# Equal destinations by ±1 products on TensorE and ScalarE, and extra bf16 matmuls into an unread PSUM bank, in a two-stage graph network

## The reference

```
h = relu(layernorm(x))                       # stage one
gate = silu(edge_attr @ W1.T + b1) @ W2.T + b2 + adapt(type[src], type[dst])
msg  = gate * h[dst] * (cutoff(edge_weight) * node_vec[dst])
agg  = segment_sum(msg, src) / clip(segment_sum(node_vec[dst], src), 1e-8)
x    = x + layernorm(h + agg) * gamma + beta
h = relu(layernorm(x))                       # stage two
h1 = relu(h @ weight1[r] + bias1);  h2 = h1 @ weight2[r]     # r: type of the edge
agg = segment_sum(h2[src, r] * norm, dst)
x   = x + relu(agg + bias2)
```

## Time and profile before

| | |
|---|---|
| median of 3 runs | 1531.99 us (1529.84 to 1539.69) |
| span of the profiled execution | 1526.4 us (the profile gives no time of its own for that launch beyond the span) |
| DVE / PE / POOL / ACT busy | 1319.3 / 1130.4 / 1026.1 / 668.1 us |
| stage one, its last adds, stage two, last pass | 0 to 689, to 743, to 1417, to 1526 us of the span |
| granted TensorE clock | two levels, 1.0 (2.4 GHz) and 0.5 (1.2 GHz), mixed in every stage |

### The profile page before, as it was taken

The page is one execution under the profiler, slowest core; times in us unless marked ns, Lnnn a source line. Parts: engine busy times, 40 slices in busy tenths (PEclk is TensorE's granted clock), DMA queues, the critical chain, the costliest instruction groups (busy, mean ns, idle before and its releaser), DMA issues.

```text
span 1526.4 us, 20418 instructions
## 1 busy us (share of the span) xinstructions
PE 1130.4 (74%) x5198; PEld 831.4 (54%) x5198; DVE 1319.3 (86%) x3932; ACT 668.1 (44%) x1627; POOL 1026.1 (67%) x809
## 2 busy tenths in 40 slices
PE   5889899989999899881068888887878887775000
PEld 2767677777777777771035555555555555554000
DVE  6999999999989998980289999998989899888599
ACT  2444444544445444540155555555555555554000
POOL 7655667777877787566667787877777777766000
PEclk9666655655556655655575656655565556666555
DMA  7999986666666656642445666555555555554899
GB/s 225 307 324 327 328 236 157 153 146 143 142 166 149 149 139 143 155 101 11 100 120 143 166 167 156 140 138 137 136 139 127 132 131 138 138 127 81 328 400 398
DMA packets 154391, 268.73 MB, mean 176 GB/s; under 512 B 73818, under 2 KB 90411, under 8 KB 153380
## 3 DMA queue, kind: packets, MB, share of 16 engines
q1 hardware_dynamic: 78228, 223.53, 43.8%
q0 software_dynamic: 68992, 24.64, 18.5%
q10 hardware_dynamic: 7056, 19.27, 3.1%
HBM read 194.33 MB, written 112.55 MB: 201 GB/s over the span
## 4 chain that ended last, share of the span: by engine, by line
PE 34%; DVE 20%; DMA 19%; POOL 12%; issue 10%; ACT 3%; SPq 1%; POOLq 0%; DVEq 0%; ACTq 0%
PE ps_m L572 10%; POOL agg L485 8%; DMA t<-agg,src_all 6%; PE ps_m L661 6%; PE ps_qs L572 6%; DMA lows<-low 4%; PE ps_k L647 3%; DVE same L858 2%; DMA agg<-y,once 2%; DMA agg<-ysq,once 2%; DVE t L1074 2%; DVE x L1070 2%; PE ps_k L559 2%; PE ps_k L560 2%; PE ps_qs L610 1%
## 5 line engine op out<-in xcount | busy, mean ns | idle before, releaser
L521 POOL DMA_INDIRECT agg<-sums,once x196 | 312.7, 1595 | 103.5 <-issue 79.8
L443 POOL DMA_INDIRECT nodes<-in_table,dst_all x196 | 194.9, 995 | 102.2 <-issue 51.7
L512 POOL DMA_INDIRECT t<-agg,src_all x196 | 191.5, 977 | 66.1 <-issue 53.9
L572 PEld LDWEIGHTS ps_m<-msg,same 128*128 128x128 f32 x980 | 200.8, 314 | 29.0 <-issue 29.0
L572 PE MATMUL ps_m<-msg,same 128*128 128x48 f32 x980 | 208.5, 398 | 1.0 <-issue 1.0
L647 PE MATMUL ps_k<-h_t,rw_sb 56*128 56x256 f32 x588 | 122.7, 536 | 114.0 <-ACT hid L742 91.3
L572 PEld LDWEIGHTS ps_qs<-msg,same 128*128 128x128 f32 x980 | 183.6, 289 | 2.1 <-DVE msg L950 2.1
L572 PE MATMUL ps_qs<-msg,same 128*128 128x49 f32 x980 | 180.7, 363 | 2.0 <-DVE msg L950 2.0
L485 POOL DMA_INDIRECT agg<-x,once x84 | 137.4, 1635 | 43.9 <-issue 21.7
L647 PEld LDWEIGHTS ps_k<-h_t,rw_sb 56*128 56x128 f32 x588 | 62.9, 242 | 157.1 <-ACT hid L742 115.2
L559 PE MATMUL ps_k<-types_lo,low_hot 128*128 128x392 bf16 x196 | 95.7, 488 | 52.7 <-DVE low_hot L833 51.0
(11 more groups left out here) (149 smaller groups left out, 2620.2 us busy)
## 6 DMA issues: line engine op xcount, KB each, us to landing
agg<-in_both SPq DMA_DIRECT2D x14, 2758.0 KB, 15.3
t<-agg SPq DMA_DIRECT2D x49, 784.0 KB, 5.3
kept<-kept_out SPq DMA_DIRECT2D x49, 404.0 KB
kept_in<-kept SPq DMA_DIRECT2D x49, 404.0 KB, 3.5
agg<-bias_rows SPq DMA_DIRECT2D x49, 384.0 KB
out<-t ACTq DMA_DIRECT2D x49, 384.0 KB, 5.8
rows<-in_src_rows SPq DMA_DIRECT2D x49, 256.0 KB, 4.2
rows<-in_dst_rows SPq DMA_DIRECT2D x49, 256.0 KB, 3.2
```

The lines of the kernel that those rows point to most:

```text
L443: pool.indirect_dma_start(nodes[s][:, t, :], None, table, bass.IndirectOffsetOnAxis(ap=dst_all[:, c:c + 1], axis=0)).then_inc(nodes_in[b % ...
L512: pool.indirect_dma_start(t2[b % T2S][:, t, :], None, wide, bass.IndirectOffsetOnAxis(ap=src_all[:, c:c + 1], axis=0)).then_inc(ends_in[b ...
L521: pool.indirect_dma_start(agg1, bass.IndirectOffsetOnAxis(ap=once1[b % LAG1][:, t:t + 1], axis=0), sums1[b % LAG1][:, t, :], None, compute ...
L572: last = mm(ps[:, t * width:(t + 1) * width], kept_same[:, at:at + P], m[:, v, :], start=(v == t), stop=(v == TILES - 1))
```

## The change

1. `keep_clock(ps, n)`: n matmuls of the bf16 identity with itself repeated, 128x512, into a PSUM bank that nobody reads (`ps_idle`, `ps_idle1`, `ps_spare`). Stage one gets ten per round, stage two six.
2. In stage two DVE no longer builds `same`. SP loads the keys of four blocks at once, each broadcast to 32 partitions; DVE shifts and masks so that partition p holds bit p mod 32 (`bits_done`), and makes it +1 or -1 in bf16 (`signs`), once in four rounds each. PE multiplies those signs (`key_dots`, contraction over 32 partitions), so that equal keys give 32; a second product adds -64 where the row's edge is later. ACT evicts with `relu(x - 31)` into `same` and sums the rows into `ahead1` (`same1_copy`).
3. Once `same` comes from ACT, `turned1` and `once1` of a block are computed one DVE round later (`d = b - 3`).

```diff
-POOL_SET = 15
+POOL_SET = 16
+GROUP = 4
+NBITS = 32
+APART = -2.0 * NBITS
...
+        signs = [upto[:, :].bitcast(BF16)[:, k * BE:(k + 1) * BE] for k in range(2)]
...
+        ps_idle = ps_k[0][:, 1, :]
+        ps_idle1 = ps_k[1][:, 1, :]
+        ps_spare = ps_k[1][:, 0, :]
+        ps_dots = [ps_k[1][:, 0, 0:P], ps_k[1][:, 0, P:3 * P], ps_k[1][:, 1, 0:3 * P], ps_k[1][:, 0, 0:BE]]
...
-            def load_rows1(b):
-                need(sp, S["same1_done"], b - 1)
-                sp.dma_start(rows[b % 2][:, :], dst_rows[b:b + 1, :].to_broadcast([P, BE])).then_inc(rows_in[b % 2], 16)
...
+            def load_keys(k):
+                need(sp, S["signs_done"], k - 1)
+                for q in range(GROUP):
+                    b = min(k * GROUP + q, NBLOCK - 1)
+                    sp.dma_start(rows[k % 2][q * NBITS:(q + 1) * NBITS, :],
+                                 dst_rows[b:b + 1, :].to_broadcast([NBITS, BE])).then_inc(keys_in[k % 2], 16)
...
+            spin = ident_bf[:, :].unsqueeze(1).to_broadcast([P, TILES, P])
+
+            def keep_clock(ps, n):
+                for _ in range(n):
+                    mm(ps, ident_bf[:, :], spin, start=True, stop=True)
...
-            def sums_within(ps, width, kept_same, m):
+            def sums_within(ps, width, kept_same, m, ps_spin):
                 for t in range(TILES):
                     for v in range(t, TILES):
+                        if v == t and t > 0:
+                            keep_clock(ps_spin, 1)
...
             for b in range(NBLOCK):
+                keep_clock(ps_idle, 3)
                 if b + 1 < NBLOCK:
                     lookup(b + 1, 0)
                     lookup(b + 1, 1)
+                keep_clock(ps_idle, 1)
...
                 last.then_inc(S["gate_done"], 1)
+                keep_clock(ps_idle, 1)
                 if b + 1 < NBLOCK:
                     h1(b + 1)
+                    keep_clock(ps_idle, 1)
                     centred(b + 1)
+                    keep_clock(ps_idle, 1)
...
+            def key_dots(b, t):
+                at = slice(b % GROUP * NBITS, (b % GROUP + 1) * NBITS)
+                bits = signs[b // GROUP % 2]
+                mm(ps_dots[t], bits[at, t * P:(t + 1) * P], bits[at, 0:(t + 1) * P], start=True, stop=False)
+                mm(ps_dots[t][:, t * P:(t + 1) * P], ident_bf[:, :], later[:, :], start=False, stop=True).then_inc(S["dots_done"], 1)
...
                         if k == 1:
-                            need(pe, S["relu1_done"], e)
+                            need(pe, S["same1_done"], TILES * e)
...
+                    need(pe, S["relu1_done"], min(e + 1, NBLOCK))
+                    sums_within(ps_sums1, H, same[f % 2], msg1, ps_idle1).then_inc(S["sums1_done"], 1)
                 if e < NBLOCK:
+                    pe.wait_ge(S["signs_done"], e // GROUP + 1)
+                    pe.wait_ge(S["relu1_done"], e + 1)
+                    for t in range(TILES - 1):
+                        key_dots(e, t)
                     need(pe, S["m1_copied"], e)
...
                     last.then_inc(S["m1_done"], 1)
+                    pe.wait_ge(S["same1_done"], TILES * e + 2)
+                    keep_clock(ps_spare, 3)
+                    key_dots(e, TILES - 1)
...
+            def same1_copy(b, t):
+                act.wait_ge(S["dots_done"], b * TILES + max(t + 1, 2))
+                if t == 0:
+                    need(act, S["sums1_done"], b - 1)
+                    need(act, S["turned1_done"], b)
+                n = P * (t + 1)
+                A(same[b % 2][:, place(t):place(t) + n], ps_dots[t], ACT.Relu, bias=1.0 - NBITS,
+                  accum_out=ahead1[:, t:t + 1]).then_inc(S["same1_done"], 1)
...
                 if 0 <= f < NBLOCK:
+                    same1_copy(f, 0)
+                    same1_copy(f, 1)
+                    same1_copy(f, 2)
                     act.wait_ge(S["m1_done"], f + 1)
...
                     nc.scalar.copy(msg1_t[:, :], ps_m[:, 0:BE // 2]).then_inc(S["m1_copied"], 1)
+                    same1_copy(f, 3)
...
-                if 0 <= d < NBLOCK:
-                    dve.wait_ge(rows_in[d % 2], 16 * (uses(NBLOCK - 1 - d % 2, 2) + uses(d, 2)))
-                    need(dve, S["sums1_done"], d - 1)
-                    same_up_to(d, dst_all, ahead1).then_inc(S["same1_done"], 1)
+                if 0 <= b < NBLOCK + GROUP - 1 and b % GROUP == 1:
+                    dve.wait_ge(S["bits_done"], b // GROUP + 1)
+                    V.tensor_scalar(signs[b // GROUP % 2], rows[b // GROUP % 2][:, :], 2.0, -1.0, ALU.mult,
+                                    ALU.add).then_inc(S["signs_done"], 1)
...
+                if 0 <= b < NBLOCK and b % GROUP == 0:
+                    k = b // GROUP
+                    dve.wait_ge(keys_in[k % 2], 16 * GROUP * uses(k, 2))
+                    need(dve, S["dots_done"], GROUP * TILES * (k - 1))
+                    V.tensor_scalar(rows[k % 2][:, :], rows[k % 2][:, :], bit_of[:, :], 1, ALU.logical_shift_right,
+                                    ALU.bitwise_and).then_inc(S["bits_done"], 1)
```

29 lines of the change are left out of this document (19 added, 10 removed).

## The result

The changed kernel takes **1625.72 us** (median of 4 runs, 1619.85 to 1631.19) against 1530.91 for the kernel before (4 runs, 1517.64 to 1539.69): ratio **1.062, 95% interval 1.056 to 1.069, slower**. Forecast were 1515 us and a range of 1484 to 1548. The profiled execution took 1630.99 us, its span is 1628.5 against 1526.4.

What follows compares the result with a forecast made beforehand. POOL's chain of adds was taken to bound stage one, a two-round loop over POOL, DVE and PE stage two. Terms -5 - 3 - 5 - 4 + 0.5 = -16.5 on 1526.4, plus 5.6, gave 1515 us, range 1484 to 1548.

Steps and rivals of the forecast that it cites:

- Item 3: Stage two's loop of two rounds: path averages 10.8 us, a round 13.2 us against 13.34, -5 us, bounds -20 and +54.
- the path of 11.07 us: Stage two, from DVE's L973 over the sums and L661 to the end of L781: 8.6 us at full clock, 13.7 at half.
- the 14.85 us to the landing: Stage two, from POOL's first add of a block over its gathers to the landing DVE awaits; kept at 14.85 us.
- Items 1 and 2: Stage one: first fourteen rounds shorten towards 12.65 us, -5 us; three more blocks of POOL's adds go at 9.46 us, -3 us.
- rival B: Nothing gained: transfers hold the first fourteen rounds, stage two's full rounds pay for the half ones; 1529 us, chance 0.19.
- Item 4: PE's own round in stage two: 10.7 us plus 4.1 at half clock, 14.8, more than the round; not added to the sum.
- Item 5: PE's waits in stage two: some 1.6 us between L661 and h2_t at full clock, hidden before the gather lands; nothing added.
- Item 6: Start and end of stage two, about two rounds where DVE's saved 1.97 us count: -4 us, bounds -6 and 0.
- C: Stage two slower: half-clock sums every round lengthen the path to 13.7 us, PE's own round to 14.8; 1574 us, chance 0.13.
- A: Clock holds in both stages, by the rule that bursts without long gaps keep full clock; -42, 1490 us, chance 0.25.
- D: Extra matmuls don't move the clock, PE bounds stage one, 4.3 us more a round; about 1780 us, chance 0.03.
- DVE's L973 no longer waits: Sign in stage two's profile for C: first adds over 13.9 us apart and no DVE wait for the gather's landing.

Runs made afterwards that it cites:

- late_all: Changed kernel with key products behind the h2 transposes, large loads held back to the next asum, and no extra matmuls; 1562.3 us, ratio 1.024.
- gap_late3: gap_late with three instead of six extra matmuls in PE's wait ahead of the last rw1 matmuls; 1639.0 us, ratio 1.073.
- loads_late: Changed kernel with loads of kept values and wide rows held back until the next round's asum has begun; 1572.4 us, ratio 1.029.
- dots_late: Changed kernel with three tiles' key products behind the h2 transposes, the last one and three extra matmuls behind the message transposes, evictions later; 1567.4 us, ratio 1.021.
- b_dots: Kernel before with the large loads held back and six bf16 key-product matmuls on constants, results unused, ahead of rw2 each round; 1563.2 us, ratio 1.029.
- s1_only: Kernel before with only stage one's ten extra bf16 matmuls a round, stage two unchanged; 1519.5 us, ratio 0.995.
- turn_first: loads_late with the h2 transposes ahead of the eviction wait, the three extra matmuls behind rw2 and the last key product; 1588.8 us, ratio 1.041.
- gap_moved: loads_late with stage two's extra matmuls replaced by six in PE's wait for relu0 ahead of the last rw1 matmuls; 1550.1 us, ratio 1.016.
- gap_late: gap_moved with the key products and evictions placed as in dots_late; 1519.6 us in one run, 1547.4 to 1560.0 in three others, no ratio given.
- split: Kernel before with stage two's sums in another PSUM bank, their copy no longer waiting for the rw2 matmuls; 1512.4 us, ratio 0.990.
- b_loads_late: Kernel before with the same held-back loads as loads_late; 1513.9 us, ratio 0.993.

## Why the prediction was wrong

- **Item 3, the path of 11.07 us, is the step that failed.** It had the ends about right, 8.6 us at full clock (9.23 in one waiting round that had it) and 13.7 at half (measured 13.56), and then took an average, 10.8. But the loop of two rounds goes through waiting rounds alone, and in these PE waits longest ahead of its sums: in all 20 rounds in which it waited 3.3 us or more ahead of L684, the sums were at half clock. The wait is not the only way to slow sums: late_all and gap_late3 have them in every round without it. The prediction even names that wait ("longer than that after which the clock was low") and still gives it half of the rounds. The rounds with fast sums have slack, and their gain went nowhere. `key_dots` was taken at 1.3 us at half clock and took 1.62, the three extra matmuls in the sums at 1.3 and took 0.87; that 13.56 is so close to 13.7 is in part these two misses against each other.
- **Also item 3: the 14.85 us to the landing were taken as fixed.** They became 14.5 to 18.7. The longer path moved the gathers against the end of `x2`, which starts 1.19 MB of loads; nothing in the sum had a row for that. loads_late prices it at 3.3 points. Taking the key products off the path was worth 4.1 (dots_late) and putting them on it cost the kernel before 3.6 (b_dots); the parts overlap and do not add up to the 6.2. Rows to ask it of were there: in the kernel before the landing already varied between 1.6 and 2.7 us by the same distance.
- **Items 1 and 2, -8 us, came to nothing.** The clock (0.89) and the rounds after the fourteenth (12.7) are as said, but the first add came at 211.47, not near 207, and the last block as before. The first fourteen rounds went only from 13.48 to 13.34 us with the DMA share at 0.96, rival B's reason (s1_only, with the same extra matmuls there, has 13.8). POOL's adds have their own pace.
- **Item 4**: PE's round is no bound; it idles 3.3 us and more ahead of L684 in most waiting rounds, 4.48 in the one shown. Only in gap_late3 did it become one.
- **Item 5, PE's queue behind L703, costed at nothing.** DVE's one-hot waits for L665 up to 2.4 us, in rounds without a landing to wait for. turn_first could not price it. ACT's row sums are an instruction of their own of 196 ns, four a round, not nothing; they run beside L703.
- **Item 6** can't be read apart.
- **The rivals.** C came true in its first mechanism, with 13.56 us for its 13.7, at a chance of 0.13. Its 1574 us lacked the landing; that loads_late, where this is gone, takes 1572 is luck, as C's loop has rounds of 14.7 us and loads_late 14.08. Its second mechanism, PE's own round as the bound, did not come. Its sign "DVE's L973 no longer waits" was wrong: DVE waited longer. A and B were out, D too. Of the rule that spoke for A: in gap_moved the clock is at half where a gap of 3.11 us is left, in gap_late, where none is, at full. In gap_late3 none is left either, and the clock is at half in all of stage two's sums, so the rule is not enough; what else decides stays open. What I failed to ask was which rounds have the gap.

## What to carry to other kernels

- If a loop's length is set by one kind of round, cost the change in that kind and not on average. Here PE's clock was at half in just the rounds in which PE had waited longest.
- When a path gets longer, list the transfers that its end or its neighbours start, and see on what they now fall. Holding large loads back until the small latency-bound gather has landed cost one wait instruction and helped both kernels.
- Work added to an idle engine is free only beside the path. Two results in one PSUM bank can put one's writer on the other's path, 1.9 us here (split); look at banks before looking at clocks.

## What the runs showed of the hardware

- In the changed kernel a gather whose last issue ended 0.8 to 1.7 us behind the start of the large loads had landed 4.2 to 6.3 us later, except once in 2.75; one that ended 0.4 to 0.7 us behind it, in 2.7 to 3.1. In the kernel before it took 2.1 to 2.7 us at 0.1 behind (once 4.7), and 1.6 to 1.9 at 0.5 ahead. With the loads held back it is 1.4 to 1.9, five times 2.2 to 2.7.
- After the wait of 4.48 us PE ran from 1102.5 to 1113.4 at 1.2 GHz (granted clock 0.50) although it was busy throughout; in the round with a wait of 0.63 us it ran at 2.4 GHz. After 2.7 us or more the sums were slow in all 20 such rounds of the changed kernel and all 16 of gap_moved. Short waits do not ensure the full clock: b_loads_late has 0.5 to 1.3 us ahead of 19 rounds' sums and all 19 are slow, late_all and gap_late3 likewise. Six bf16 matmuls of 512 columns take 1.47 us at the full clock and 2.74 in gap_late, where they begin at half.
- ACT's row sum is a separate instruction of 0.19 to 0.21 us in the changed kernel, beside an eviction of 0.27 to 0.60 us (128 to 512 columns).
- Two patterns of clock can each last through all of stage two: sums of 2.43 us in every round of gap_late's trace, of 4.50 in every round of gap_late3's, with three small matmuls a round between the two programs. With one trace of each, and gap_late's own times from 1519.6 to 1560.0, that these three decide it is likely, not shown.
